# Attention mix scaled by inverse row sums sent through DRAM, and the second layer norm of a tile in the last slot

## What is computed

```python
q, k, v = jnp.einsum('bsx,xMnd->Mbnsd', x, qkv)        # x (4,1024,128), qkv (128,3,16,64)
a = jnp.einsum('bnsd,bntd->bnst', q, k) * 64 ** -0.5
a = jax.nn.softmax(a + bias, axis=-1)                  # causal; bias by distance
mix = jnp.einsum('bnst,bntd->bnsd', a, v)
x = layernorm(x + jnp.einsum('bnsd,ndx->bsx', mix, out_w))
r = sigmoid(xr @ W_r.T); k_act = square(relu(xk @ W_k.T))   # xr, xk: mixes of x and the token before
x = layernorm(x + r * (k_act @ W_v.T))
```

## Time and profile before

| | |
|---|---|
| median of 3 runs | 1245.46 us (1243.8 to 1245.8) |
| the profiled execution, its own time | 1246.39 us |
| span of its instructions | 1244.6 us |
| granted PE clock over the span (mean) | 0.988 |
| busy share: PE, PEld, DVE, ACT, POOL | 90%, 63%, 68%, 60%, 71% |
| period of a step without a tile, with a tile | 34.4 us, 37.5 us |

### The profile page before, as it was taken

The page is one execution under the profiler, slowest core; times in us unless marked ns, Lnnn a source line. Parts: engine busy times, 40 slices in busy tenths (PEclk is TensorE's granted clock), DMA queues, the critical chain, the costliest instruction groups (busy, mean ns, idle before and its releaser), DMA issues.

```text
span 1244.6 us, 21976 instructions
## 1 busy us (share of the span) xinstructions
PE 1118.1 (90%) x6909; PEld 781.9 (63%) x6909; DVE 843.3 (68%) x2505; ACT 743.1 (60%) x1857; POOL 886.9 (71%) x527
## 2 busy tenths in 40 slices
PE   5899999999999999999999999999999999999885
PEld 3666666666666666666666666666666666666664
DVE  2666666666676767777667777666777676777746
ACT  3666666666655656656665656665656566656623
POOL 1877777878876677876677876677876677776730
PEclk9899999999999999999999999999999999999997
DMA  8855445555655455655465654456654455654600
GB/s 199 208 122 124 115 117 122 130 132 134 157 138 115 116 141 127 160 137 129 116 141 132 159 127 118 117 140 153 159 123 115 123 134 142 155 122 110 213 18 20
DMA packets 101745, 163.69 MB, mean 132 GB/s; under 512 B 10592, under 2 KB 66288, under 8 KB 101632
## 3 DMA queue, kind: packets, MB, share of 16 engines
q1 hardware_dynamic: 99472, 161.37, 53.4%
q10 hardware_dynamic: 2160, 0.92, 0.3%
HBM read 41.63 MB, written 19.96 MB: 49 GB/s over the span
## 4 chain that ended last, share of the span: by engine, by line
PE 65%; DVE 17%; issue 8%; ACT 6%; POOL 2%; DMA 1%; DVEq 0%; SPq 0%; ACTq 0%
PE ps_o L946 21%; PE ps_t L930 15%; PE ps_rows L916 13%; PE ps_m L891 7%; DVE prob L615 4%; DVE pt L632 4%; PE ps_m L960 4%; PE ps_m L896 3%; ACT pt L474 2%; DVE mix_sb L638 2%; POOL prob L410 2%; ACT prob L463 1%; DVE k_lo L601 1%; DVE q_lo L601 1%; DVE shift L682 1%
## 5 line engine op out<-in xcount | busy, mean ns | idle before, releaser
L410 POOL TENSOR_SCALAR prob<-prob,inv 128x128 f32<-128x128 f32 (+7 forms) x512 | 880.5, 1730 | 308.2 <-DVE inv L622 306.2
L463 ACT ACTIVATE prob<-prob,low 128x128 f32<-128x128 f32 (+7 forms) x512 | 395.3, 773 | 119.1 <-DVE low L615 116.9
L615 DVE CUSTOM_DVE_ANT_0 prob<-ps_rows,table 128x128 f32<-128x128 f32 (+7 forms) x512 | 383.6, 749 | 72.7 <-PE ps_rows L916 66.2
L930 PE MATMUL ps_t<-ident,prob 128*128 128x128 f32 x2304 | 349.1, 278 | 87.2 <-ACT pt L474 50.1
L916 PE MATMUL ps_rows<-stacks 128*128 128x512 f32 (+3 forms) x1536 | 402.5, 372 | 4.6 <-DVE w_t L700 3.2
L930 PEld LDWEIGHTS ps_t<-ident,prob 128*128 128x128 f32 x2304 | 260.6, 141 | 198.3 <-issue 130.6
L632 DVE COPY pt<-ps_t 128x256 f32<-128x256 f32 (+2 forms) x320 | 179.1, 568 | 179.6 <-PE ps_t L930 178.8
L474 ACT ACTIVATE pt<-ps_t 128x128 f32<-128x128 f32 (+2 forms) x448 | 203.6, 477 | 110.8 <-PE ps_t L930 110.6
L946 PE MATMUL ps_o<-pt,v_pair 128*64 128x512 f32 (+3 forms) x1536 | 268.7, 492 | 0.0
L916 PEld LDWEIGHTS ps_rows<-stacks 128*128 128x128 f32 x1536 | 246.3, 191 | 22.7 <-DVE w_t L700 3.4
L946 PEld LDWEIGHTS ps_o<-pt,v_pair 128*64 128x64 f32 x1536 | 101.8, 136 | 181.8 <-issue 172.3
(11 more groups left out here) (108 smaller groups left out, 561.6 us busy)
## 6 DMA issues: line engine op xcount, KB each, us to landing
stacks<-k_hi SPq DMA_DIRECT2D x126, 256.0 KB, 4.7
stacks<-k_lo SPq DMA_DIRECT2D x126, 256.0 KB, 4.9
stacks<-q_hi SPq DMA_DIRECT2D x63, 256.0 KB, 3.7
stacks<-q_lo SPq DMA_DIRECT2D x63, 256.0 KB, 4.4
mix_transposed<-mix_sb SPq DMA_DIRECT2D x62, 256.0 KB, 2.0
table<-bias_by_distance SPq DMA_DIRECT2D x64, 192.0 KB, 3.7
mix_tile<-mix_transposed SPq DMA_DIRECT2D x24, 512.0 KB, 5.0
w_cur<-in_L_attn_qkv SPq DMA_DIRECT2D x31, 192.0 KB, 3.9
```

Source lines behind the costliest of these rows:

```text
L410: nc.gpsimd.tensor_scalar(row, row, inv[:, r:r + 1], None, ALU.mult).then_inc(s_norm, 1)
L463: nc.scalar.activation(row, row, ACT.Exp, bias=low[:, r:r + 1], scale=-1.0, accum_out=total[:, r:r + 1]).then_inc(s_exp, 1)
L615: nc.vector.tensor_tensor_reduce(prob[:, r % PSLOTS, 0:width], ps_rows[:, score_at(r):score_at(r) + width], table[n % 2][:, h, 0:width][:, ...
L930: ins = nc.tensor.transpose(ps_t[k % 2][:, P * b:P * b + P], prob[:, r % PSLOTS, at:at + P], ident[:, :])
```

## The change

POOL no longer normalises the rows. The rows are transposed and mixed as they come from the exponential, and the mix is scaled afterwards: `store_mix` multiplies `ps_o` by `inv_all` (64 partitions a head, one column a query, each the inverse sum of that query). To get there, DVE takes the reciprocals of 8 rows at once (slots 5 and 12), PE transposes these [128, 8] into the free last quarter of bank 6 and bank 19, DVE (bank 6) and ACT (bank 19) copy the [8, 128] to `inv_t`, SP stores it in DRAM (4 KB), waits for that store, and reads it back twice with one source for 64 partitions (128 KB a read). The store and the read of a group stand at different places of SP's order: for group 0 the store ahead of `stack_k` and the reads behind it; for group 1 the store late in the step and the reads early in the next. Besides, the second layer norm of a tile (ACT's two instructions and DVE's one) goes from slot 13 to slot 15.

```diff
-V_PROJ, LN2_RSTD, LN2 = 12, 13, 13
+V_PROJ, LN2_RSTD, LN2 = 12, 15, 15
+INV_READY = (5, 12)
+INV_BANK = (6, 19)
+            def store_inverse(n, g):
+                sp.wait_ge(s_inv_t[g], n + 1)
+                sp.dma_start(inv_d[n % 2, g, :, :], inv_t[g][:, :]).then_inc(s_inv_d[g], 16)
+            def spread_inverse(n, g):
+                sp.wait_ge(s_inv_d[g], 16 * n + 16)
+                if n > 0:
+                    sp.wait_ge(s_o, 2 * n + g)
+                for h in range(2):
+                    sums = inv_d[n % 2, g, GROUP * h:GROUP * h + GROUP, :].rearrange("(a i) q -> a (i q)", a=1)
+                    sp.dma_start(inv_all[g][D * h:D * h + D, :], sums.broadcast_to([D, GROUP * P]))\
+                        .then_inc(s_inv_all[g], 16)
...
-            for n in range(PAIR_STEPS):
-                for r in range(NROWS):
-                    normalise(n, r)
...
+                if n > 0 and r % (2 * GROUP) == 0:
+                    act.wait_ge(s_inv, 2 * n - 1 + r // (2 * GROUP))
...
-            def invert(n, r):
-                dve.wait_ge(s_exp, NROWS * n + r + 1)
-                nc.vector.reciprocal(inv[:, r:r + 1], total[:, r:r + 1]).then_inc(s_inv, 1)
+            def invert(n, g):
+                rows = slice(2 * GROUP * g, 2 * GROUP * (g + 1))
+                dve.wait_ge(s_exp, NROWS * n + 2 * GROUP * (g + 1))
+                if n > 0:
+                    dve.wait_ge(s_tr, NBANKS * n + INV_BANK[g] + 1)
+                nc.vector.reciprocal(inv[:, rows], total[:, rows]).then_inc(s_inv, 1)
...
-                nc.vector.tensor_copy(mix_sb[g][:, :], ps_o[:, :]).then_inc(s_o, 1)
+                dve.wait_ge(s_inv_all[g], 32 * n + 32)
+                nc.vector.tensor_tensor(mix_sb[g][:, :], ps_o[:, :], inv_all[g][:, :], ALU.mult).then_inc(s_o, 1)
...
-                pe.wait_ge(s_norm, NROWS * n + r + 1)
+                pe.wait_ge(s_exp, NROWS * n + r + 1)
...
+                    if k in INV_BANK:
+                        g = INV_BANK.index(k)
+                        pe.wait_ge(s_inv, 2 * n + g + 1)
+                        ins = nc.tensor.transpose(ps_t[k % 2][0:2 * GROUP, 3 * P:],
+                                                  inv[:, 2 * GROUP * g:2 * GROUP * (g + 1)], ident[:, :])
```

More of the change, by code:

```diff
@@ L94, in build @@
     mix_d = nc.dram_tensor("mix_transposed", (PAIR_STEPS, P, SEQ), F32, kind="Internal").ap()
+    inv_d = nc.dram_tensor("inverse_sums", (2, 2, 2 * GROUP, P), F32, kind="Internal").ap()
     xt_d = nc.dram_tensor("x_transposed", (BATCH, P, SEQ), F32, kind="Internal").ap()
@@ L130, in build @@
         inv = sb("inv", [P, NROWS])
+        inv_t = [sb(f"inv_t{g}", [2 * GROUP, P]) for g in range(2)]
+        inv_all = [sb(f"inv_all{g}", [P, GROUP * P]) for g in range(2)]
         pt = [[sb(f"pt{h}{g}", [P, GROUP * (g + 1), GROUP * P]) for g in range(2)] for h in range(2)]
@@ L203, in build @@
         s_inv = sem("inverted")
-        s_norm = sem("normalised")
+        s_inv_t = [sem(f"inverse_transposed{g}") for g in range(2)]
+        s_inv_d = [sem(f"inverse_in_dram{g}") for g in range(2)]
+        s_inv_all = [sem(f"inverse_broadcast{g}") for g in range(2)]
         s_tr = sem("transposed")
@@ L350, in step @@
                     load_weights(n + 2)
+                if prev:
+                    spread_inverse(n - 1, 1)
                 if more:
@@ L364, in step @@
                     store_mix(n - 1, 1)
+                store_inverse(n, 0)
                 if more:
@@ L368, in step @@
                         stack_k(n + 1, h, s_stack[h])
+                spread_inverse(n, 0)
                 if n + 1 >= TILE_LAG:
@@ L373, in step @@
                 store_mix(n, 0) if more else None
+                store_inverse(n, 1)
                 if (n + 2) % PAIRS == 0 and n + 2 < PAIR_STEPS:
@@ L379, in _ @@
             drive(step)
+            spread_inverse(PAIR_STEPS - 1, 1)
             tile_store(PAIR_STEPS - TILE_LAG)
@@ L473, in evacuate @@
                 act.wait_ge(s_tr, NBANKS * (n + 1) + k + 1)
+                if k == INV_BANK[1]:
+                    if n > 0:
+                        act.wait_ge(s_inv_d[1], 16 * n)
+                    nc.scalar.activation(inv_t[1][:, :], ps_t[k % 2][0:2 * GROUP, 3 * P:], ACT.Copy).then_inc(s_inv_t[1], 1)
                 nc.scalar.activation(pt[h][g][:, b0:b0 + nb, P * (i % GROUP):P * (i % GROUP) + P],
@@ L631, in evacuate @@
                 dve.wait_ge(s_tr, NBANKS * (n + 1) + k + 1)
+                if k == INV_BANK[0]:
+                    if n > 0:
+                        dve.wait_ge(s_inv_d[0], 16 * n)
+                    nc.vector.tensor_copy(inv_t[0][:, :], ps_t[k % 2][0:2 * GROUP, 3 * P:]).then_inc(s_inv_t[0], 1)
                 nc.vector.tensor_copy(pt[h][g][:, b0:b0 + nb, P * (i % GROUP):P * (i % GROUP) + P],
@@ L707, in step @@
                         bias(*row)
-                    for row in rows_ahead(n, more, slot - 1):
-                        invert(*row)
+                    if slot in INV_READY:
+                        invert(n, INV_READY.index(slot))
                     if more and slot in PROJ_SLOTS[:4]:
```

2 lines of the change are left out of this document (removed).

## The result

| | before | after |
|---|---|---|
| median | 1244.83 us (1243.8 to 1245.8, 4 runs) | **1283.29 us** (1279.59 to 1289.97, 4 runs) |
| ratio, 95% interval | | 1.0315 [1.0269, 1.0361] |
| profiled execution, span | 1246.39, 1244.6 us | 1279.59, 1277.9 us |
| granted PE clock over the span | 0.988 | 0.981 |
| period without a tile (mean of 6) | 34.39 us | 34.98 us |

The change costs 38.5 us, where 22 were forecast. The periods are distances between the group-0 scalings (before: copies) of successive steps in the timeline. The profiled execution is the fastest of the four.

A forecast was written before the change was run, and what follows sets the result against it. PE, 90% busy, was taken as the bound, with tile steps ending in a chain over DVE and ACT. 1246.4 + 13.2 + 4.5 - 1.5 + 5.5 = 1268 us; own range 1255 to 1280, 0.8 range 1240 to 1298.

The forecast's parts named there:

- What bounds the kernel: PE is busy 90% of the span; POOL releases nobody, and a tile step ends in a chain over DVE and ACT.
- Rival 4: POOL released PE after all: the 60.7 us of weight-load waits come back, near 1200 us; chance 0.02.
- The moved norm: ACT's wait for DVE's statistics ahead of banks 18 and 19 goes: up to 0.69 us in 23 tile steps, 16 us.
- Transposes, copies, stores, group 1: Added work on PE, DVE, ACT and SP: nothing while PE's waits last; 8 us for the transposes without them.
- The arrival of group 0's sums: Reads land 1.0 us behind the last `k_lo`; scaling starts at 671.2 instead of 669.22, tile step 0.6 us longer.
- break-even: Arrival of group 0's sums at 670.6, from bank 20's start at 673.25 less 2.67 us.
- Bank 20 behind the scaling: On DVE in a tile step, bank 20 starts 2.67 us behind the scaling, where it was 4.03.
- the shorter L715: With POOL silent, this DVE instruction, before L682 at 0.64 us, takes near 0.3 us; 0.35 us off a tile step's chain.
- No-tile steps: In 9 steps with `stack_k` but no tile, bank 20 starts at 198.9 against 198.44: 0.5 us each, 4.5 us.
- The clock: PE idle behind the held-back v projection: one clock fall in a quarter of 22 steps, 1.0 us each, 5.5 us.
- rival 3: Clock falls in most tile steps, or partitions reading the same bytes run below 197 GB/s: 1291 us; chance 0.2.
- Rivals 1 and 2: Sums land with the stacks, 1235 us, chance 0.16; or they arrive near 670.6 to 670.8, 1246 us, chance 0.08.

The follow-up runs named there:

- norm_only: Kernel before with only the second norm moved from slot 13 to 15, POOL normalising as before; 1223.21 us, ratio 0.9839.
- no_pool: Kernel before without POOL's scaling of the softmax rows, second norm at its old place, division by row sums left out; 1236.33 us, ratio 0.9940.
- norm_no_pool: Kernel before without POOL's scaling of the softmax rows and with the second norm in slot 15; 1221.91 us, ratio 0.9828.
- no_reads0: Changed kernel without the two group-0 reads a step, first half of each mix multiplied by ones; 1223.63 us, ratio 0.9835.
- busy_after: Changed kernel with bank 19's two blocks transposed four times instead of once in each tile step; 1271.24 us, ratio 1.0211.
- busy_sums: Changed kernel with the second norm back in slot 13 and six transposes more in each tile step; 1302.4 us, ratio 1.0472.
- after_again: Changed kernel run once more, unaltered, as the measure for the runs with added transposes; 1285.43 us, ratio 1.0335.
- pool_reads: Changed kernel with the two group-0 reads issued from POOL's queue once their store has landed; 1229.0 us, ratio 0.9880.

## Why the prediction was right or wrong

- **What bounds the kernel: right.** POOL releases nobody, by norm_only, no_pool and norm_no_pool. Rival 4 is refuted: near 1200 it would have been, 1236 and 1222 it is.
- **The moved norm: right, and somewhat low.** 16 us were forecast, 21 measured in the medians, of which the profiled periods show 0.8 x 22 = 18.
- **Transposes, copies, stores, group 1: right.** Costed at nothing; no_reads0 is 1.7 us above norm_no_pool, within the spread of the runs. The transposes of the sums stand where PE waits anyway.
- **The arrival of group 0's sums: right in mechanism, mis-sized.** From the step's last `k_lo` instruction on DVE to the scaling the forecast has 13.74 us (671.2 against 657.46), measured are 14.04 (672.24 to 686.28). The term that was mis-sized is the 1.0 us for two reads behind the last stack: they landed 1.3 us behind it. SP's own two issues of them took 2.24 us in the queue, and the sums released DVE 0.3 us later than assumed. Since every us behind the break-even counts whole, the quiet tile period is 38.5 us, not 38.1: 22 x 0.4 = 9 us, all of what the prediction allowed for this rate on one side.
- **Bank 20 behind the scaling: right**, 2.71 us for 2.67; and the shorter L715, 0.29 us, which the Trainium skill (SBUF — State Buffer, SBUF: two separate sides) would put down to a port pair that GpSimd and DVE operations with two SBUF operands take in turn. The traces agree: 0.63 us in the median with POOL at work, 0.29 in all 24 cases of no_pool and of the changed kernel.
- **No-tile steps: right.** 0.5 us forecast; the mean of six is 0.59, and without the one of 36.1 us among them 0.4.
- **The clock: mis-sized.** 5.5 us were counted, as a fall in a quarter of 22 steps; nine of 22 have one, and such a period is 1.1 to 1.7 us longer (2.7 where the stretch at 0.50 was twice as long), not 1.0: 14 us by busy_after, 12 by the periods of the profiled execution. The place was named rightly: PE idle behind the held-back v product. It is a narrow thing: steps of the same execution with and without a fall differ by tenths of a us in DVE's wait, and not always the way one would think (a fall at 2.02, none at 2.42). The executions spread with it: the changed kernel took 1279.59 us at a mean granted clock of 0.981 and 1289.97 at 0.974, busy_sums 1294.5 at 0.991 and 1311.31 at 0.973. In number the nine falls are nearer to the quarter of 22 that was taken than to rival 3's nearly all; in time 1283 is nearer to that rival's 1291 than to 1268, as the falls were dearer and the reads later than counted.
- **Together**: 1283 lies above the 1255 to 1280 that the forecast gave as its own and inside of the wider range. 1268 + 9 + 8.5 = 1285.5. The startup gave 2.6 us (first scaling at 55.13, where the copy was at 57.70), which is luck of this execution: its clock didn't fall there, while in after_again it fell twice and the first scaling came at 58.2. The stretch behind the last scaling that waits for its reads, that of step 30, gave 3.2 us where 1.5 were forecast. That makes 1281, against 1279.6 of the profiled execution; the median lies 3.7 us above that one.
- **Rivals 1 and 2** needed the sums to land at most 0.4 to 0.6 us behind the last stack. They landed 1.3 us behind it (686.1 against 684.8). The same reads from another queue (pool_reads) came in time.

## What to carry to other kernels

A small transfer is as late as the queue that it stands in: here 256 KB behind 2 MB, and the two reads cost 60 us where everything else that was added cost about 2. Before taking load off an engine, ask who waits for it. POOL was 71% busy and worth 1 to 7 us, while one instruction pair that kept two copies waiting on ACT was worth 21. And a wait that leaves TensorE idle can cost more in clock: here 14 us on top of 46, which transposes without use in the gap gave back.

## What the runs showed that was not expected

- That six added transposes a tile step keep the granted clock full and make a kernel 14 us faster.
- The length of PE's gap does not tell which steps lose the clock: it fell behind gaps of 1.36 and 1.90 us and stayed behind gaps of 1.57 and 1.76 us. The Trainium skill (TensorE: Matmul & The Clock Gate, HAM oscillation) blames longer single gaps than any of these. Page and measurement differ, and the measurement decides.
- Reads of 128 KB whose source is one row for 64 partitions landed 2.7 us after issue at best, 3.6 in the median and 5.6 at worst.
- From POOL the same reads went through a queue of their own, and made the other queue's stacks 1.1 us later.
